# Causal attention on one core: the products for scores, maxima and q as four matmul tiles of 32 rows by 32 columns instead of one of 32 by 128

## The reference, cut to what matters

```python
Q = embeddings @ W_Q
K = embeddings @ W_K
V = embeddings @ W_V
scale = 1.0 / jnp.sqrt(jnp.float32(d))                    # d = 32
scores = jnp.einsum('bqd,bkd->bqk', Q, K) * scale
masked = jnp.where(causal[None, :, :], scores, -jnp.inf)  # 3136 x 3136 per image, 16 images
probs = jax.nn.softmax(masked, axis=-1)
return jnp.einsum('bqk,bkd->bqd', probs, V)
```

## Time and profile before

| what | value |
|---|---|
| time before, median of 2 runs | 4702.2 us (4697.58 to 4706.83) |
| the profiled execution, its own time | 4710.27 us |
| its span, first to last instruction | 4708.6 us |
| busy: TensorE / weight loads / VectorE / ScalarE / GpSimd | 88% / 61% / 67% / 58% / 30% |
| mean granted TensorE clock | 0.942 of 2.4 GHz |
| causal attention L2 / L3, first to last matmul of a bank | 1559 to 2983 us / 3127 to 4546 us |

### The profile page before, as it was taken

One profiled execution on the slowest core, in us unless ns is written; L12 is line 12 of the kernel. 1 busy time (PEld: TensorE's weight loads), 2 busy tenths in 40 slices (PEclk: granted clock), 3 DMA queues, 4 the chain that ended last, 5 costly groups with the idle time before them and its releaser, 6 DMA issues. The chain is left out here.

```text
span 4708.6 us, 125775 instructions
## 1 busy us (share of the span) xinstructions
PE 4141.0 (88%) x51290; PEld 2867.8 (61%) x51290; DVE 3134.4 (67%) x6164; ACT 2752.3 (58%) x5706; POOL 1430.2 (30%) x2222
## 2 busy tenths in 40 slices
PE   3888888888686799999999999779999999999975
PEld 2666666666332466666676666456666666666754
DVE  4777777777798466666666666536666666666653
ACT  2777777776586355655655555415555556556541
POOL 4333223321000343433433432122433434334220
PEclk9999999999798699999999999769999999999987
DMA  1200000000000000000000000000000000000003
GB/s 25 33 3 3 2 2 3 2 2 2 3 1 1 1 2 2 2 2 3 2 3 2 2 2 2 6 1 2 2 2 2 3 2 2 2 2 2 3 6 55
DMA packets 348272, 24.07 MB, mean 5 GB/s; under 512 B 346388, under 2 KB 347700, under 8 KB 347700
## 3 DMA queue, kind: packets, MB, share of 16 engines
q1 hardware_dynamic: 347700, 16.03, 4.7%
HBM read 7.88 MB, written 6.42 MB: 3 GB/s over the span
## 5 line engine op out<-in xcount | busy, mean ns | idle before, releaser
L561 DVE TENSOR_REDUCE L2a_mx<-L2a_r 128x1 f32<-128x512 f32 (+4 forms) x1344 | 760.8, 627 | 243.4 <-PE L2a_r L425 240.3
L561 DVE TENSOR_REDUCE L3a_mx<-L3a_r 128x1 f32<-128x512 f32 (+4 forms) x1344 | 760.5, 627 | 239.8 <-PE L3a_r L425 236.4
L529 ACT ACTIVATE L2a_e<-L2a_r 128x512 f32<-128x512 f32 (+3 forms) x1344 | 658.8, 579 | 284.9 <-PE L2a_r L404 282.7
L529 ACT ACTIVATE L3a_e<-L3a_r 128x512 f32<-128x512 f32 (+3 forms) x1344 | 658.6, 579 | 280.5 <-PE L3a_r L404 278.5
L425 PE MATMUL L2a_r<-L2a_vT,L2a_qT 32*128 32x512 f32 (+3 forms) x3488 | 817.6, 529 | 0.0
L425 PE MATMUL L3a_r<-L3a_vT,L3a_qT 32*128 32x512 f32 (+3 forms) x3488 | 815.0, 528 | 0.1
L404 PE MATMUL L2a_r<-L2a_qT,L2a_vT 32*128 32x512 f32 (+4 forms) x3488 | 779.8, 518 | 29.4 <-DMA L2a_qT<-L2a_nm 29.4
L404 PE MATMUL L3a_r<-L3a_qT,L3a_vT 32*128 32x512 f32 (+4 forms) x3488 | 777.6, 516 | 27.3 <-DMA L3a_qT<-L3a_nm 27.3
L1454 POOL TENSOR_SCALAR win_xw<-win_xr,win_mv,win_rs 32x343 f32<-32x343 f32 (+7 forms) x432 | 327.9, 779 | 703.3 <-ACT win_rs L1242 703.2
L404 PEld LDWEIGHTS L2a_r<-L2a_qT,L2a_vT 32*128 32x128 f32 x3488 | 372.1, 188 | 189.3 <-issue 100.3
L404 PEld LDWEIGHTS L3a_r<-L3a_qT,L3a_vT 32*128 32x128 f32 x3488 | 370.6, 187 | 186.8 <-issue 98.9
(11 more groups left out here) (370 smaller groups left out, 6745.0 us busy)
## 6 DMA issues: line engine op xcount, KB each, us to landing
L2a_qT<-L2a_nm SPq DMA_DIRECT2D x768, 0.5 KB, 2.0
L3a_qT<-L3a_nm SPq DMA_DIRECT2D x768, 0.5 KB, 2.0
T<-in_x SPq DMA_DIRECT2D x16, 384.0 KB, 3.7
out<-T SPq DMA_DIRECT2D x16, 384.0 KB, 4.0
win_mq<-win_nmt SPq DMA_DIRECT2D x256, 3.1 KB, 1.7
win_msk<-in_L_conv_pos_emb SPq DMA_DIRECT2D x49, 0.2 KB
L2a_qT<-L2a_nm SPq DMA_DIRECT2D x32, 0.2 KB, 1.8
L3a_qT<-L3a_nm SPq DMA_DIRECT2D x32, 0.2 KB, 1.8
```

The costliest lines, as they stand in the source:

```text
L529: nc.scalar.activation(E[0:r, n % RE, 0:w], bank_of(x)[0:r, 0:w], ACT.Exp).then_inc(exp_done, 1)
L561: return nc.vector.tensor_reduce(to, frm, AX.X, ALU.max)
```

## The change

Each call of lines 404, 425 and 463 becomes four calls. Each takes 32 of the 128 stationary columns and the same moving operand and writes 32 of the 128 partitions of the same bank (two calls where a key tile has 64 keys). Only the last of an item signals, as before. The other products, the order of the items, the banks and the waits are as they were.

```diff
                         for u, c0, c1, o in bank:
                             r = rows(u)
-                            last = nc.tensor.matmul(bank_of(x)[0:r, o:o + c1 - c0],
-                                                    VT[g0:g0 + C, img % 2, u * P:u * P + r],
-                                                    QT_[g0:g0 + C, img % 2, j * QB + c0:j * QB + c1],
-                                                    start=True, stop=True)
+                            for k0 in range(0, r, C):
+                                last = nc.tensor.matmul(bank_of(x)[k0:k0 + C, o:o + c1 - c0],
+                                                        VT[g0:g0 + C, img % 2, u * P + k0:u * P + k0 + C],
+                                                        QT_[g0:g0 + C, img % 2, j * QB + c0:j * QB + c1],
+                                                        start=True, stop=True)
                         last.then_inc(s_full, 1)
...
                         def dots(o, q0, c0, c1, start=True, stop=True):
-                            return nc.tensor.matmul(bank_of(x)[:, o:o + c1 - c0], QT_[g0:g0 + C, img % 2, q0:q0 + P],
-                                                    VT[g0:g0 + C, img % 2, c0:c1], start=start, stop=stop)
+                            for p0 in range(0, P, C):
+                                tile = nc.tensor.matmul(bank_of(x)[p0:p0 + C, o:o + c1 - c0],
+                                                        QT_[g0:g0 + C, img % 2, q0 + p0:q0 + p0 + C],
+                                                        VT[g0:g0 + C, img % 2, c0:c1], start=start, stop=stop)
+                            return tile
...
-                        nc.tensor.matmul(bank_of(x)[:, 0:w], A[:].rearrange("p r c -> p (r c)"),
-                                         VT[0:C, img % 2, f * QB:f * QB + w],
-                                         start=True, stop=True).then_inc(item_full, 1)
+                        for g in range(QT):
+                            last = nc.tensor.matmul(bank_of(x)[g * C:g * C + C, 0:w], A[:, g],
+                                                    VT[0:C, img % 2, f * QB:f * QB + w],
+                                                    start=True, stop=True)
+                        last.then_inc(item_full, 1)
```

## The result

The changed kernel takes **4979.4 us** (two runs, 4978.42 and 4980.41) against 4702.2: a ratio of **1.059, 95% interval 1.054 to 1.064**. It is slower by 277 us. The prediction was 4674 us, with a range up to 4850. The profiled execution of the changed kernel has a span of 4976.7 us, 268 us more than before.

A forecast was written before the change was run, and what follows sets the result against it. VectorE was taken to set the pace inside stretches, TensorE alone at the seams between them. Terms of -19 - 6 - 7 - 6 + 10 = -28 us took 4710.3 to 4682, less 8 for the runs' median: 4674 us, range 4590 to 4850.

The forecast's parts named there:

- the supply of instructions: First set of a stretch, 64 instead of 16 instructions: a cost of 0.03 us x 320, +10 us, at most 80.
- Rival 3: No gain: the next bank's loads are held up by waiting instructions, 32 to 64 us over 320 stretches, 4722 us; chance 0.14.
- End of a stretch: Last maxima bank before pv: its exposed load gets shorter, 0.06 us x 320, -19 us, all on the path.
- start: Start of a stretch: the third bank, the first that VectorE gets, comes 0.02 us earlier x 320, -6 us.
- q: The 224 q products, each nearly alone after a wait: 0.06 us each, between 0 and 13 us, -7 us taken.
- Edge banks: Four pieces of 128 columns, two passes each: loads last as long as streaming, 32-column loads free little; nothing taken.
- Tail: Sets with 64-column passes: shorter loads let streaming decide, at most 16 us gained, at least nothing; -6 us taken.
- Rival 1: Slower: TensorE can't be fed instructions fast enough, tail first; 4831 us at 12 ns, about 5090 at 18 ns; chance 0.18.
- Rival 2: Slower by far: the tiles of a bank run one after another, 2.15 us a bank, 5900 us; chance 0.07.
- Rival 4: Faster: every bank's exposed load counts, inside stretches too, if TensorE's latency binds the sets; 94 us, 4585 us; chance 0.12.

The follow-up runs named there:

- run 10: Changed kernel, four tiles of 32 columns, with the maxima of the last two diagonal pieces of every full edge bank left out: 4986.4 us, ratio 1.0579.
- run 15: Changed kernel's four tiles of 32 columns, with each set's maxima banks written ahead of its score banks: 4863.9 us, ratio 1.0319 against the kernel before.
- run 8: Kernel before, with only the three sets an image that hold the tail's scores in four tiles of 32 columns: 4797.5 us, ratio 1.0166.
- run 11: Kernel before, with q alone in four tiles of 32 columns, scores and maxima as they were: 4840.3 us, ratio 1.0265.
- run 5: Changed kernel with two tiles of 64 columns instead of four, each 512-column call cut into two of 256: 4708.1 us, ratio 0.9984 against the kernel before.
- run 2: Changed kernel with scores, maxima and q as two tiles of 64 columns instead of four of 32: 4669.4 us, ratio 0.9903 against the kernel before.
- run 12: Changed kernel with two tiles of 64 columns, each 512-column call cut into four of 128: 6042.4 us, ratio 1.2801 against the kernel before.
- run 6: Changed kernel with two tiles of 64 columns in sets holding an edge bank or tail scores, four elsewhere: 4882.0 us, ratio 1.0353 against the kernel before.
- run 3: Changed kernel with only the maxima in four tiles, scores and q back in one call of 128 columns: 6875.7 us, ratio 1.459 against the kernel before.

## Why the prediction was wrong

**The step that failed** is the cost of "the supply of instructions", taken at +10 us and at most 80, together with Rival 3. The prediction asked at what rate instructions arrive, and never how many TensorE can hold. Rival 3 had the mechanism, "a bank has four times as many instructions that wait ahead of the next bank's loads", but at 0.1 to 0.2 us for each of 320 stretches, 4722 us. The runs show 0.6 to 1.0 us in each of the five other segments and 1.8 to 2.6 us in the tail's: 5.5 to 6.3 us an image, 175 to 200 us. For W, the held passes of the changed trace, run 10 and run 15 are the direct evidence. How much of the 5.5 to 6.3 us it accounts for is not shown for every segment: it puts VectorE's first reading 0.47 us late in five of the six.

- **Clock.** The prediction kept the clock as it was. Half-clock time rose from 2.8 to 8.4 us an image and goes with 70 to 95 us. It rose in run 8, where only the tail stalls, as well. That the stalls let the clock fall is argued, not shown; no run holds the clock.
- **End of a stretch, -19 us, and start, -6 us.** The product is shorter as worked out (loads of 104 ns, first passes of 0.61 us), but hardly anything came of it: two tiles leave segments 0, 1 and 3 at 7.00, 9.61 and 5.81 us. The step took the last maxima bank's start as fixed. It is set by when VectorE frees the bank, and VectorE's first reading, of the edge bank, begins no earlier (1.66 us after the mask against 1.62); that this is the reason is argued.
- **q, -7 us.** 0.06 us where q stands alone, as predicted (run 11). The sum over an image can't be read apart from the rest.
- **Edge banks, nothing taken.** Here lay 0.47 us in each of five segments, 2.3 us of an image: 64 instructions of 128 columns behind two score banks.
- **Tail, -6 us of at most 16.** Right for two tiles and too small: 0.76 us an image, 24 us. For four it was of the wrong sign, since it counted 192 instructions for the set and asked only for 7.5 ns each, and not for room for them.
- **Rival 1.** Tiles in after start 7 ns apart when queued and 17 ns apart (four instructions) behind a stall, about 4 ns for an instruction. The supply was faster than assumed. Its times, 4831 and about 5090, lie on both sides of the measured one, for a wrong reason; runs 5 and 15 exclude it as the main cause. (Its sum has seven sets with an edge bank in an image; there are six, since the tail's is a single product.)
- **Rival 2.** Excluded: the first passes of a bank's four tiles start within 0.02 us (2172.28 to 2172.30), and where four banks start together, their 16 first passes start within 0.10 us (1711.96 to 1712.06 in L2).
- **Rival 4.** Excluded by run 2, where shorter loads gained nothing in segments 0, 1 and 3: inside a stretch VectorE set the pace.
- **The range** to 4850 left out the true value because its dear end was built from a rate alone, Rival 1's.

## What to carry to other kernels

Before cutting a product into tiles, count the loads and matmuls (two pairs for each fp32 call) from the oldest one that hasn't ended: past 64, free rows and columns of the array stay empty. Split as far as the exposed load pays, here two tiles, put what the busiest reader waits for first in the order, and keep one tile width among the banks that run side by side. A busy share near 100% hides a stall of this kind; the distance between starts and the reader's first instruction after a fixed mark show it.

## What the runs showed of the hardware that was not expected

- At most 64 loads and matmuls are held, taken in by program order: the 65th starts 0.03 us after the pass at their head ends, at either clock (2172.92 behind a pass of 0.61 us; 4032.03 behind one of 1.06 us).
- A tile takes at most three waiting pairs of load and matmul before the stream behind it stops, for other tiles too (run 12, ratio 1.28, and the kernel before at 2124.16). Inferred from these two places.
- A change of tile width lets the array run empty: 0.62 us at one border (run 6), ratio 1.46 where widths alternate within a set (run 3).
